# Expert stage of a graph and feed-forward kernel: first weights copied to fixed places, and a ring of four output buffers

## The chip, the cores and the metric

The kernel runs on one core of a Trainium2 chip. The metric is the device time of one execution in microseconds (us). The kernel before takes 2433.99 us, the median of three runs (2428.54 to 2436.15).

The engines are named as the profile names them: PE is TensorE's matmul and PEld its weight load, DVE is VectorE, ACT is ScalarE, POOL is GpSimd, SP is the engine that issues most DMAs. A name with a q behind it (SPq, POOLq) is the instruction queue of that engine.

## The reference

Two parts run one after the other on 3125 nodes with 256 features each.

```
x = x + gnn(layernorm(x))            # 4 layers of a relational graph network, 100000 edges
x = x + ffn(layernorm(x))            # a mixture of 8 experts, 2 for each node

def ffn(x):                          # E = 8 experts, D = 256, H = 512
    xn = layernorm(x) * gamma + beta
    top_vals, top_idx = top_k(xn @ Wr + br, 2)
    w = softmax(top_vals)
    for e in range(E):
        h   = gelu(xn @ W1[e] + b1[e])          # 256 -> 512
        y_e = h @ W2[e] + b2[e]                 # 512 -> 256
        y  += y_e * (w of expert e, 0 where the node did not choose it)
```

Only the second part, and in it only the experts and what follows them, is touched here.

## The kernel before, in words

The graph layers and the routing fill the first 2140 us. The router gives every chosen pair of node and expert a row in a table XG in device memory, sorted by expert; an expert's rows are padded up to a multiple of 128. A row holds the node's normalized features as a high and a low float16 half and, behind them, the number of the row of the output table YG to which its result goes. Padding rows hold number 0, and row 0 of YG is read by nobody; node n owns rows 1 + 2n and 2 + 2n.

The expert stage works on NB = 56 blocks of 128 rows. Each block has one expert, known only on the chip, so its weights are addressed through a register (`bass.ds(at, ...)`). Both weight tables lie in SBUF for all 8 experts, 2048 float16 columns each: W1HL and W2HL. For a block b the engines do this:

- SP loads the 128 rows of XG into XB (4 buffers, L1224). It waits until the block four before has been transposed and until its output row numbers have been copied.
- PE `turn(b)` transposes the four 128x128 pieces (L2104); ACT `turned(b)` takes them to SBUF (L1361).
- PE `up(b)` (L2115) makes 24 matmuls of 128x128 with weights from W1HL. Here the weights are the stationary operand, and its address is dynamic.
- ACT applies Gelu in four pieces (L1375) and makes the high half of the result (L1381). DVE makes the low half (L2080, semaphore `hl`).
- PE `down(b)` (L2130) makes 12 matmuls with 256 columns. Stationary is the hidden value, at a fixed address; W2HL is the moving operand, at a dynamic address.
- DVE `down_evac(b)` (L2067) scales, adds b2 and writes YB, which has 2 buffers.
- POOL (L1424) writes YB to the rows of YG by an indirect DMA, whose row numbers DVE has copied into IDX (L2078, 4 columns).

The order on each engine is written out by hand. PE does turn(b+1), up(b), down(b-2). ACT does turned(b+1), Gelu(b), high half(b). DVE does the row numbers of b, the low half of b, the evacuation of b-2. POOL issues the write of b when `ybv` says that the evacuation is done and, from the second on, when the write of b-1 has landed (`yb0` or `yb1`). DVE takes the row numbers of b only when the write of b-4 has landed, and evacuates b-2 only when b-4 has.

When all writes have landed, SP reads YG back, 25 tiles of 125 nodes (L1229, two DMAs each), DVE adds the two weighted results of each node to X (L1563, L1566), and ACT's queue stores the tile. DVE waits for the loads in groups of tiles: 0 and 1, then four at a time from 2 to 21, then 22 to 24.

The program holds a second kernel for other graphs (the Dense classes and functions). It isn't executed with this input.

Of the kernel before, what the change touches and what calls it, by code (L numbers as in the profile page):

```python
# [7 lines left out]
F32 = mybir.dt.float32  # L8
# [652 lines left out]
class Memory:  # L661


    def __init__(self, nc, ctx, c):
# [3 lines left out]
        def dram(name, shape, dt):  # L668
            return nc.dram_tensor(f"n_{name}", shape, dt).ap()
# [448 lines left out]
def sync_program(e, a, c, m, s):  # L1118
# [271 lines left out]
def gpsimd_program(e, a, c, m, s):  # L1390
# [66 lines left out]
def vector_program(e, done, a, c, m, s):  # L1457
# [257 lines left out]
def tensor_program(e, a, c, m, s):  # L1715
# [12 lines left out]
    for what, l, i in c.order:  # L1728
# [53 lines left out]
        elif what == "rd":  # L1782
# [233 lines left out]

def blocks_vector(e, q, c, m, s):

    bq, bt, ti = m.bc[0:TN], m.bt, m.ti

# [38 lines left out]
    def expert(b, w):  # L2059
        return e.snap(regs[w][b // GB % 2][b % GB], min_val=0, max_val=(E8 - 1) * (1, 256)[w])  # L2060

    def down_evac(b):
        e.wait_ge(s["dn"], b + 1)
        e.wait_ge(s["b2"], 16) if b == 0 else None
        if b >= 2:
            e.wait_ge(s[f"yb{b % 2}"], 16 * (b // 2))
        e.scalar_tensor_tensor(m.YB[:, b % 2, :], m.bank(3 + b % 3, 0, D), m.FSC[:, 1, bass.ds(expert(b, 0), 1)],  # L2067
                               m.B2F[:, bass.ds(expert(b, 1), D)], ALU.mult, ALU.add).then_inc(s["ybv"], 1)

    for b in range(NB + 2):  # L2070
        if b < NB:
            if b % GB == 0:
                for w in range(2):
                    e.reg_load(regs[w][b // GB % 2], ti[0:1, (2, 4)[w], b:b + GB])
            e.wait_ge(s[f"xb{b % 4}"], 16 * (b // 4 + 1))
            if b >= 4:
                e.wait_ge(s[f"yb{b % 2}"], 16 * ((b - 4) // 2 + 1))
            e.tensor_copy(m.IDX[:, b % 4:b % 4 + 1], m.XB[:, b % 4, 2 * D:RW].bitcast(I32)).then_inc(s["idx"], 1)  # L2078
            e.wait_ge(s["hh"], b + 1)
            e.scalar_tensor_tensor(m.HHL[:, b % 3, 1, :], m.H[:, b % 2, :], m.fsc[:, bass.ds(expert(b, 0) + 24, 1)],  # L2080
                                   m.HHL[:, b % 3, 0, :], ALU.mult, ALU.subtract).then_inc(s["hl"], 1)
        if b >= 2:
            down_evac(b - 2)


def experts(e, c, m, s, n_whl):
    e.wait_ge(s["posd"], c.routes)
# [7 lines left out]
    def expert(b):  # L2095
        return e.snap(regs[b // GB % 2][b % GB], min_val=0, max_val=(E8 - 1) * 2048)
# [10 lines left out]
    def up(b):  # L2107
        e.wait_ge(s["xbt"], b + 1)
        if b >= 3:
            e.wait_ge(s["gl"], b - 2)  # L2110
        at = expert(b)
        for k4 in range(4):
            for k in range(2):
                for w, x in ((0, 0), (0, 1), (1, 0)):
                    ins = e.matmul(m.bank(b % 3, 128 * k4, 128),  # L2115
                                   m.W1HL[:, bass.ds(at + (1024 * k + 512 * w + 128 * k4), 128)],
                                   m.XBT[:, b % 2, 128 * (2 * x + k):128 * (2 * x + k) + 128],
                                   start=(k == 0 and w + x == 0), stop=(k == 1 and w == 1))
        ins.then_inc(s["up"], 1)
# [196 lines left out]
class DenseMemory:  # L2316


    def __init__(self, nc, ctx, c):
# [169 lines left out]
def dense_sync(e, a, c, m, s):  # L2489
# [104 lines left out]
def dense_scalar(e, a, c, m, s):  # L2594
# [317 lines left out]
def dense_vector(e, a, c, m, s):  # L2912
# [122 lines left out]
def dense_tensor(e, a, c, m, s):  # L3035
# [207 lines left out]
```

## Time and profile before

| what | us |
|---|---|
| median of the runs shown | 2433.99 |
| span of the profiled execution, first to last instruction | 2411.0 |
| PE busy | 2037.9 (85%) |
| DVE busy | 1593.9 (66%) |
| ACT busy | 800.7 (33%) |
| POOL busy | 1363.9 (57%) |
| mean granted TensorE clock | 0.940 of full speed |
| first and last start of L2115, the up matmuls | 2146.7 and 2351.2 |
| first and last start of L1424, the output writes | 2162.1 and 2370.7 |
| first start of L1229, the reading back | 2373.9 |

The profile states no time of its own for the profiled execution other than the span. The runs shown are 23 us longer than the span: that is what lies before the first and behind the last instruction, and the change doesn't touch it.

A busy share is an average over the whole kernel, and this change touches the last 265 us. So the views that matter are the timeline, the chain of waits and the busy times of that stretch. Each waiting instruction is put down to the one that ended last before it; where an engine is never put down as waiting, its own pace is the limit.

### The profile page before, as it was taken

How to read it: one execution, taken by the hardware profiler on the slowest of the kernel's cores; microseconds unless marked ns; L12 is line 12 of the kernel's file. 1: busy time of each engine (PE TensorE's matmuls, PEld its weight loads, DVE VectorE, ACT ScalarE, POOL GpSimd, SP SyncE). 2: the span in 40 equal slices, each digit the busy share in tenths (PEclk: the TensorE clock that was granted, in tenths of full speed). 3: DMA queues.
4: the chain of work that ended last, by engine and by line, in shares of the span. 5: the costliest groups of instructions: out<-in, count | busy, mean ns of one | idle time of the engine just before them, and what ended most of it. 6: DMA issues, size and time to landing. Idle time of an engine off the chain costs nothing. (4 is left out here: it accounts for less than half of the span.)

```text
span 2411.0 us, 48597 instructions
## 1 busy us (share of the span) xinstructions
PE 2037.9 (85%) x16548; PEld 1310.3 (54%) x16548; DVE 1593.9 (66%) x5383; ACT 800.7 (33%) x1632; POOL 1363.9 (57%) x1344
## 2 busy tenths in 40 slices
PE   0576998999988989889999999889999998559990
PEld 0334655665555556556655565554665655348780
DVE  5986877877866567676646776763677777543334
ACT  1665656665541111111111221210122112137770
POOL 2034554646450777777467777764777777722230
PEclk9988999999999999999999999999999998669995
DMA  5599554535553787776579777756776564332225
GB/s 154 156 276 296 149 147 127 163 118 186 148 153 88 257 235 257 238 222 209 179 244 270 243 255 236 249 175 216 260 239 207 184 205 118 98 99 72 70 73 174
DMA packets 215194, 448.63 MB, mean 186 GB/s; under 512 B 42478, under 2 KB 138722, under 8 KB 213287
## 3 DMA queue, kind: packets, MB, share of 16 engines
q1 hardware_dynamic: 136023, 261.82, 35.1%
q0 software_dynamic: 67168, 172.52, 23.7%
q10 hardware_dynamic: 11760, 11.08, 1.7%
q8 instruction: 147, 2.41, 0.4%
q14 instruction: 96, 0.79, 0.1%
HBM read 344.26 MB, written 100.70 MB: 185 GB/s over the span
## 5 line engine op out<-in xcount | busy, mean ns | idle before, releaser
L1402 POOL DMA_INDIRECT n_BIG<-n_xd,n_SIDX x1200 | 1226.5, 1022 | 768.6 <-PE n_PS L1891 307.7
L1870 PE MATMUL n_PS<-n_BIG 125*128 125x500 f16 x4400 | 1059.8, 377 | 14.7 <-DVE n_BIG L1536 12.3
L1870 PEld LDWEIGHTS n_PS<-n_BIG 125*128 125x128 f16 x4400 | 392.6, 98 | 361.4 <-issue 15.4
L1891 PE MATMUL n_PS<-n_OW,n_BIG 128*128 128x116 f16 (+24 forms) x4800 | 352.7, 207 | 112.6 <-DMA n_BIG<-n_xd,n_SIDX 110.8
L1891 PEld LDWEIGHTS n_PS<-n_OW,n_BIG 128*128 128x128 f16 x4800 | 290.2, 99 | 278.7 <-DMA n_BIG<-n_xd,n_SIDX 147.4
L1911 PE MATMUL n_PS<-n_BIG,n_tabs 128*128 128x256 f16 x2400 | 295.8, 283 | 0.0
L1582 DVE TENSOR_TENSOR n_ST<-n_PS,n_INVB 128x500 f32<-128x500 f32 x200 | 200.3, 1043 | 125.1 <-issue 65.3
L1911 PEld LDWEIGHTS n_PS<-n_BIG,n_tabs 128*128 128x128 f16 x2400 | 244.7, 102 | 36.9
L1491 DVE TENSOR_SCALAR n_OW<-n_io,n_tabs 128x116 f16<-128x116 f16 (+24 forms) x1200 | 213.1, 270 | 57.6 <-PE n_PS L1891 57.4
L1608 DVE SCALAR_TENSOR_TENSOR n_U<-n_PS,n_cw,n_BI 125x256 f32<-125x256 f32 x100 | 48.1, 481 | 256.5 <-PE n_PS L1911 256.0
L1304 ACT ACTIVATE n_U<-n_U 125x256 f32<-125x256 f32 x100 | 41.4, 414 | 517.5 <-DVE n_U L1618 487.2
L1293 ACT ACTIVATE n_tabs<-n_ST 128x1000 f16<-128x1000 f32 x100 | 103.7, 1037 | 325.5 <-DVE n_ST L1582 295.4
L1277 ACT ACTIVATE n_BIG<-n_PS 128x500 f16<-128x500 f32 x275 | 150.5, 577 | 136.1 <-PE n_PS L1841 135.4
L1841 PE MATMUL n_PS<-n_BIG,n_tabs 128*128 128x400 bf16 (+4 forms) x576 | 134.8, 338 | 28.2 <-DVE n_tabs L1483 10.9
L1424 POOL DMA_INDIRECT n_yg<-n_BIG,n_IDX x56 | 59.9, 1069 | 172.8 <-DMA n_yg<-n_BIG,n_IDX 146.8
L1478 DVE TENSOR_SCALAR n_BIG<-n_io,n_tabs 128x400 bf16<-128x400 f16 (+4 forms) x576 | 147.9, 309 | 8.1 <-PE n_PS L1841 8.1
L1504 DVE TENSOR_TENSOR n_tabs<-n_ST,n_tabs 128x1000 f16<-128x1000 f32 x100 | 119.7, 1197 | 30.5 <-ACT n_tabs L1293 30.4
L2115 PE MATMUL n_PS<-n_BIG 128*128 128x128 f16 x1344 | 114.7, 226 | 0.3
L1284 ACT ACTIVATE n_XT<-n_PS 128x500 f16<-128x500 f16 x100 | 58.5, 586 | 155.3 <-PE n_PS L1753 155.2
L1258 ACT ACTIVATE n_tabs<-n_io,n_tabs 128x125 bf16<-128x125 f16 x288 | 91.2, 390 | 44.6 <-PE n_PS L1841 44.3
L2115 PEld LDWEIGHTS n_PS<-n_BIG 128*128 x1344 | 92.5, 99 | 18.4 <-issue 2.2
L1375 ACT ACTIVATE n_BIG<-n_PS,n_B1T,n_FSC 128x128 f32<-128x128 f32 x224 | 84.4, 457 | 43.7 <-PE n_PS L2115 41.2
(275 smaller groups left out, 2219.4 us busy)
## 6 DMA issues: line engine op xcount, KB each, us to landing
n_BIG<-n_a SPq DMA_DIRECT2D x160, 625.0 KB, 5.5
n_a<-n_BIG SPq DMA_DIRECT2D x11, 3125.0 KB, 12.2
n_xg<-n_tabs SPq DMA_DIRECT2D x53, 481.9 KB, 10.1
n_INVB<-n_ind SPq DMA_DIRECT2D x100, 250.0 KB
n_BIG<-n_xd,n_SIDX POOLq DMA_INDIRECT x1200
n_BIG<-in_L_ffn_W_dram SPq DMA_DIRECT2D x32, 512.0 KB, 4.7
n_xd<-n_BIG SPq DMA_DIRECT2D x75, 112.0 KB
n_whl<-n_BIG SPq DMA_DIRECT2D x16, 512.0 KB
```

Source lines behind the costliest of these rows:

```text
L1277: e.activation(rows[:, :, 20 * g:20 * g + 20], m.bank(4 + c.unit_of["block", i], 0, W).rearrange("p (q k) -> p k q", k=T), ACT.Copy).then_ ...
L1293: e.activation(m.SH[i % 2 if l else 0][:, 0, :, :, 0:TN], m.ST, ACT.Copy).then_inc(s["shi"], 1)
L1402: e.indirect_dma_start(m.GR[:, g % GS, :], None, m.XD[l % 2][:, :], bass.IndirectOffsetOnAxis(ap=m.SIDX[:, i:i + 1], axis=0)).then_inc(s[f ...
L1478: e.tensor_scalar(m.OC[i % S][:, at], m.io[:, at], m.VS[:, i:i + 1], None, ALU.is_equal).then_inc(s["oc"], 1)
L1491: e.tensor_scalar(c.window(m, w)[0], m.io[:, 0:c.width[w]], m.SCOL[:, w:w + 1], None, ALU.is_equal).then_inc(s["win_made"], 1)
L1504: e.tensor_tensor(lo, m.ST, hi, ALU.subtract).then_inc(s["slo"], 1)
L1582: ins = e.tensor_tensor(m.ST[:, h], m.bank(2 * p + h, 0, W).rearrange("p (n r) -> p r n", r=R), m.INVB[:, k, :].rearrange("p (n r) -> p r ...
L1841: e.matmul(m.bank(4 + c.unit_of["block", g])[:, at], m.OS[b % 3][:, i % 4, :], m.OC[i % S][:, at], start=(j == 0), stop=(j + 1 == c.groups ...
L1870: ins = e.matmul(m.bank(2 * p + h, 0, W), m.xps[l % 2][0:TN, part, D * k + 128 * h:D * k + 128 * h + 128], m.RA[0:TN, c.slot_of(n), W * (k ...
L1891: ins = e.matmul(m.bank(2 * p + h, at, c.width[q]), m.GR[:, g % GS, D * part + 128 * h:D * part + 128 * h + 128], ow, start=False, stop=Fa ...
L1911: ins = e.matmul(out, sums[:, x, h, r, :], m.WH[:, l % 2, w, h, r, :], start=False, stop=(x == 1 and h == 1 and r == R - 1))
L2115: ins = e.matmul(m.bank(b % 3, 128 * k4, 128), m.W1HL[:, bass.ds(at + (1024 * k + 512 * w + 128 * k4), 128)], m.XBT[:, b % 2, 128 * (2 * x ...
```

## The change

It has four parts, all in the expert stage and in what follows.

1. A ring W1R of W1S = 4 places with fixed addresses, in SBUF that the graph layers have left. DVE copies the 2048 columns of a block's first weights from W1HL to place b % 4 (`w1_copy`), three blocks before the loop and in it, and then at the start of iteration b for block b+2. PE's `up(b)` waits for the copy (`w1_put`) and reads the ring. The copy waits until the up matmuls of the place's last user are done.
2. YB has YS = 4 buffers, in other memory, with four semaphores. POOL no longer waits for the write of b-1; DVE evacuates block b when the write of b-4 has landed. The row numbers still wait for the write of b-4.
3. YG has 4 spare rows ahead of the nodes' rows. A padding row's number becomes b % 4 (a maximum with b % 4), by one instruction in place of the copy.
4. The groups of tiles that DVE waits for at the end begin at tiles 0, 3, 8, 13 and 19: five groups, where it had seven.

```diff
+LOADED = (3, 8, 13, 19)
+YS = 4
+W1S = 4
...
+        self.W1R = BIG[:, 0:2048 * W1S].rearrange("p (b h) -> p b h", b=W1S)
...
-        self.YB = xpf[:, 5120:5632].rearrange("p (b d) -> p b d", b=2)
+        self.YB = raf[:, 4096:4096 + YS * D].rearrange("p (b d) -> p b d", b=YS)
...
 for b in range(NB):                                   # POOL
     e.wait_ge(s["ybv"], b + 1)
-    if b:
-        e.wait_ge(s[f"yb{(b - 1) % 2}"], 16 * ((b - 1) // 2 + 1))
     e.indirect_dma_start(m.YG[:, :], bass.IndirectOffsetOnAxis(ap=m.IDX[:, b % 4:b % 4 + 1], axis=0),
-                         m.YB[:, b % 2, :], None).then_inc(s[f"yb{b % 2}"], 16)
+                         m.YB[:, b % YS, :], None).then_inc(s[f"yb{b % YS}"], 16)
...
+    def w1_copy(b):                                   # DVE
+        if b % GB == 0:
+            e.reg_load(wide[b // GB % 2], ti[0:1, 1, b:b + GB])
+        if b >= W1S:
+            e.wait_ge(s["up"], b - W1S + 1)
+        at = e.snap(wide[b // GB % 2][b % GB], min_val=0, max_val=(E8 - 1) * 2048)
+        e.tensor_copy(m.W1R[:, b % W1S, :], m.W1HL[:, bass.ds(at, 2048)]).then_inc(s["w1_put"], 1)
+
+    if ring:
+        e.wait_ge(s["whl"], 16 * 12)
+        for b in range(W1S - 2):
+            w1_copy(b)
     for b in range(NB + 2):
         if b < NB:
+            if ring and b + W1S - 2 < NB:
+                w1_copy(b + W1S - 2)
...
             if b >= 4:
-                e.wait_ge(s[f"yb{b % 2}"], 16 * ((b - 4) // 2 + 1))
-            e.tensor_copy(m.IDX[:, b % 4:b % 4 + 1], m.XB[:, b % 4, 2 * D:RW].bitcast(I32)).then_inc(s["idx"], 1)
+                e.wait_ge(s[f"yb{b % ys}"], 16 * ((b - 4) // ys + 1))
+            rows_of = m.XB[:, b % 4, 2 * D:RW].bitcast(I32)
+            if ring:
+                e.tensor_scalar(m.IDX[:, b % 4:b % 4 + 1], rows_of, float(b % YS), None, ALU.max).then_inc(s["idx"], 1)
...
-        at = expert(b)                                # PE, up(b)
+        if ring:
+            e.wait_ge(s["w1_put"], b + 1)
...
+                    col = 1024 * k + 512 * w + 128 * k4
                     ins = e.matmul(m.bank(b % 3, 128 * k4, 128),
-                                   m.W1HL[:, bass.ds(at + (1024 * k + 512 * w + 128 * k4), 128)],
+                                   m.W1R[:, b % W1S, col:col + 128] if ring else m.W1HL[:, bass.ds(at + col, 128)],
```

On PE, the rows of one block from its transposes to its second matmuls. L2096 works out the block's register, ISA are register instructions, BIG holds the weights and PS is PSUM. Before:

```order
L2104 MATMUL n_PS<-n_idh,n_tabs 128x128 x3
L2096 ISA [waits gl,xbt]
L2115 MATMUL n_PS<-n_BIG 128x128 x2
L2115 ISA
L2115 MATMUL n_PS<-n_BIG 128x128
L2115 ISA
L2115 MATMUL n_PS<-n_BIG 128x128 x2
```

The pattern goes on until 24 matmuls are through. Now:

```order
L2132 MATMUL n_PS<-n_idh,n_tabs 128x128 x3
L2147 MATMUL n_PS<-n_BIG 128x128 [waits w1_put,gl,xbt]
L2147 MATMUL n_PS<-n_BIG 128x128 x23
L2124 ISA [waits hl]
L2162 MATMUL n_PS<-n_BIG 128x256
L2162 ISA
```

The 15 register instructions between the up matmuls are gone, and the one ahead of them; those of the down matmuls stay. A wait on `w1_put` has come in.

On DVE, one iteration of the loop, from the row numbers to the next row numbers. Before:

```order
L2078 COPY n_IDX<-n_tabs 128x1 [waits yb1,xb1]
L2060 ISA [waits hh]
L2080 SCALAR_TENSOR_TENSOR n_BIG<-n_BIG,n_fi 128x512
L2060 ISA [waits yb1,dn]
L2067 REGISTER_ALU
L2067 SCALAR_TENSOR_TENSOR n_BIG<-n_PS,n_FSC,n_BIG 128x256
L2078 COPY n_IDX<-n_tabs 128x1 [waits yb0,xb2]
```

Now:

```order
L2104 TENSOR_SCALAR n_IDX<-n_tabs 128x1 [waits yb1,xb1]
L2068 ISA [waits hh]
L2108 SCALAR_TENSOR_TENSOR n_BIG<-n_BIG,n_fi 128x512
L2068 ISA [waits dn]
L2075 REGISTER_ALU
L2075 SCALAR_TENSOR_TENSOR n_BIG<-n_PS,n_FSC,n_BIG 128x256
L2082 TENSOR_LOAD n_BIG
L2085 ISA [waits up]
L2086 COPY n_BIG<-n_BIG 128x2048
L2104 TENSOR_SCALAR n_IDX<-n_tabs 128x1 [waits yb2,xb2]
```

Between the evacuation and the next row numbers stands the copy of 128x2048, with the load of four block offsets (L2082) once in four blocks. In the first blocks the evacuation waits for no write.

## Rows read from the trace of the kernel before

**Rows 1.** Busy time by stretch: us, then PE, PEld, DVE, ACT, POOL, clock, DMA share, GB/s

```profile
2155.30:2349.40 194.10, 191.56 (x2119) 157.44 (x2118) 67.64 (x156) 144.79 (x322) 53.67 (x51) 1.00 0.23 71
```

**Rows 2.** Waits from 2155.3 to 2349.4: engine, line, releaser, us in total, times, longest

```profile
POOL n_yg L1424 <- DMA n_yg<-n_BIG,n_IDX: 130.7, 49, 4.4
...
PE n_PS L2104 <- DMA n_tabs<-n_xg: 0.6, 1, 0.6
```

**Rows 3.** DMA issues from 2155.3 to 2349.4: count, median us to landing

```profile
n_yg<-n_BIG,n_IDX POOLq DMA_INDIRECT x51, 2.7
```

**Rows 4.** Timeline, 2298 to 2310: start, us, engine, line, operation

```profile
2299.14 1.76 PEld L2115 LDWEIGHTS n_PS<-n_BIG 128*128 x24
...
2301.06 1.22 PEld L2130 LDWEIGHTS n_PS<-n_BIG 128*128 128x128 f16 x12
...
2304.66 1.50 PE L2130 MATMUL n_PS<-n_BIG 128*128 x12
...
2306.22 1.91 PE L2115 MATMUL n_PS<-n_BIG 128*128 128x128 f16 x24
```

**Rows 5.** Timeline, 2154.5 to 2162.2, the third and fourth block

```profile
2155.33 1.51 ACT L1375 ACTIVATE n_BIG<-n_PS,n_B1T,n_FSC 128x128 f32<-128x128 f32 x4 [1.64 <-PE n_PS L2115]
2155.38 2.12 PE L2115 MATMUL n_PS<-n_BIG 128*128 128x128 f16 x24
2156.98 0.72 ACT L1381 ACTIVATE n_BIG<-n_BIG,n_fi 128x512 f16<-128x512 f32 x1
...
2157.87 0.75 DVE L2080 SCALAR_TENSOR_TENSOR n_BIG<-n_BIG,n_fi 128x512 f16<-128x512 f32 x1 [3.69 <-ACT n_BIG L1381]
...
2158.81 1.16 PEld L2115 LDWEIGHTS n_PS<-n_BIG 128*128 x20
```

**Rows 6.** DVE's groups by shape, whole kernel: busy us, mean ns | idle before

```profile
L1478 DVE TENSOR_SCALAR n_BIG<-n_io,n_tabs 128x500 bf16<-128x500 f16 x186 | 64.6, 351 | 8.1 <-PE n_PS L1841 8.1
...
L1478 DVE TENSOR_SCALAR n_BIG<-n_io,n_tabs 128x100 bf16<-128x100 f16 x83 | 20.1, 249 | 0.0
...
L1519 DVE SCALAR_TENSOR_TENSOR n_BIG<-n_BIG,n_wb 128x2048 f16<-128x2048 f32 x4 | 9.4, 2350 | 4.4 <-ACT n_BIG L1298 4.4
...
L2078 DVE COPY n_IDX<-n_tabs 128x1 int32<-128x1 int32 x56 | 8.6, 154 | 116.8 <-DMA n_yg<-n_BIG,n_IDX 113.2 <-DMA n_tabs<-n_xg 3.6
```

**Rows 7.** Line 1491, whole kernel: count: ns min/median/max, first and last start

```profile
L1491 DVE TENSOR_SCALAR n_OW<-n_io,n_tabs x1200: 210/244/691, 120.5 to 2090.6; 128x104 f16<-128x104 f16 x13, 128x124 f16<-128x124 f16 x11, 128x92 f16<-128x92 f16 x9, 128x120 f16<-128x120 f16 x9
```

**Rows 8.** Line 1402, whole kernel, the same columns

```profile
L1402 POOL DMA_INDIRECT n_BIG<-n_xd,n_SIDX x1200: 940/946/3237, 113.8 to 2104.2; - x172
```

**Rows 9.** Timeline, 2348.9 to 2352, the last block's up matmuls

```profile
2349.45 2.01 PE L2115 MATMUL n_PS<-n_BIG 128*128 128x128 f16 x24
```

**Rows 10.** Timeline, 2350 to 2411, from the last Gelu to the last tile

```profile
2351.63 1.51 ACT L1375 ACTIVATE n_BIG<-n_PS,n_B1T,n_FSC 128x128 f32<-128x128 f32 x4 [0.97 <-PE n_PS L2115]
...
2356.02 0.75 DVE L2080 SCALAR_TENSOR_TENSOR n_BIG<-n_BIG,n_fi 128x512 f16<-128x512 f32 x1
...
2356.93 1.74 PE L2130 MATMUL n_PS<-n_BIG 128*128 x12 [2.35 <-DVE n_BIG L2080]
...
2373.88 21.83 SPq L1229 DMA_DIRECT2D n_BIG<-n_yg  x50
...
2394.74 0.48 DVE L1563 SCALAR_TENSOR_TENSOR n_X<-n_BIG,n_INVA,n_X 125x256 f32<-125x256 f32 x1 [0.57 <-DMA n_BIG<-n_yg]
...
2398.95 0.48 DVE L1563 SCALAR_TENSOR_TENSOR n_X<-n_BIG,n_INVA,n_X 125x256 f32<-125x256 f32 x1 [0.46 <-DMA n_BIG<-n_yg]
...
2404.97 0.48 DVE L1566 SCALAR_TENSOR_TENSOR n_X<-n_BIG,n_INVA,n_X 125x256 f32<-125x256 f32 x1
```

**Rows 11.** Chain of waits, 2344 to 2411: start, us, what

```profile
2355.82 0.71 issue
2356.52 4.99 DMA n_yg<-n_BIG,n_IDX
...
2370.69 3.12 DMA n_yg<-n_BIG,n_IDX
```

More of the change, by code:

```diff
@@ L59 @@
 xo0 xo1 x1 xn xh_hi xh_lo xh_iota xh rxt xnt lg sm2 rexp sel rpos posd pos_made
-cnt_mm bi_made ti_made b2 xbt_mm xbt up gl hh hl dn ybv idx y_last out""".split()
+cnt_mm bi_made ti_made b2 w1_put xbt_mm xbt up gl hh hl dn ybv idx y_last out""".split()
 NEARS += [f"slot{i}" for i in range(6)] + [f"row{i}" for i in range(GS)] + [f"scat{i}" for i in range(XHS)]
-NEARS += [f"xb{i}" for i in range(4)] + [f"yb{i}" for i in range(2)] + [f"g{i}" for i in range((T + 1) // 4 + 1)]
+NEARS += [f"xb{i}" for i in range(4)] + [f"yb{i}" for i in range(YS)] + [f"g{i}" for i in range(len(LOADED) + 1)]
 DENSES = """padded edges x_in consts pool_const ev r0 gathered gp_tr vs b1 b1_tr ln hi0 xp oc os slot_free evac
@@ L677, in __init__ @@
         self.MW = dram("mw", (L, 128), F32)
-        self.YG = dram("yg", (1 + 2 * N, D), F32)
+        self.YG = dram("yg", (YS + 2 * N, D), F32)
+        self.y_rows = self.YG[YS:, :]
         self.AD = dram("a", (c.TD, 128, T * W), F16)
@@ L891, in prep_gpsimd @@
     k.did(e.memset(m.onef[:, :], 1.0))
-    k.did(e.iota(m.rows[:, :], [[1, 2]], base=1, channel_multiplier=2))
+    k.did(e.iota(m.rows[:, :], [[1, 2]], base=YS, channel_multiplier=2))
     k.did(e.memset(m.mh[:, :], -0.5))
@@ L1224, in sync_program, with wait_outputs_ready, load_group @@
         e.dma_start(m.XB[:, b % 4, :], m.XG[bass.ds(row, 128), :]).then_inc(s[f"xb{b % 4}"], 16)
-    wait_outputs_ready(e, s)
+    wait_outputs_ready(e, s, YS)
     for t in range(T):
         for p, n in ROWS:
-            e.dma_start(m.two(t)[p:n].rearrange("p j d -> p (j d)"), gathered(m, t)[p:n]).then_inc(s[f"g{(t + 2) // 4}"], 16)
+            e.dma_start(m.two(t)[p:n].rearrange("p j d -> p (j d)"), gathered(m, t)[p:n]).then_inc(s[f"g{load_group(t)}"], 16)
     e.wait_ge(s["out"], 32 * T)
-def wait_outputs_ready(e, s):
+def wait_outputs_ready(e, s, ys):
     e.wait_ge(s["dn"], NB)
-    for i in range(2):
-        e.wait_ge(s[f"yb{i}"], 16 * (NB // 2))
+    for i in range(ys):
+        e.wait_ge(s[f"yb{i}"], 16 * (NB // ys))
+def load_group(t):
+    return sum(1 for first in LOADED if t >= first)
 def gathered(m, t):
-    return m.YG[1:1 + 2 * N, :].rearrange("(n j) d -> n (j d)", j=2)[TN * t:TN * t + TN]
+    return m.y_rows.rearrange("(n j) d -> n (j d)", j=2)[TN * t:TN * t + TN]
 def scalar_program(e, a, c, m, s):
@@ L1557, in vector_program @@
             places(e, q, m, s, i)
-    blocks_vector(e, q, c, m, s)
+    blocks_vector(e, q, c, m, s, True)
     for t in range(T):
-        e.wait_ge(s[f"g{(t + 2) // 4}"], 32 * sum(1 for i in range(T) if (i + 2) // 4 == (t + 2) // 4))
+        e.wait_ge(s[f"g{load_group(t)}"], 32 * sum(1 for i in range(T) if load_group(i) == load_group(t)))
         both, n = m.two(t), c.place[L - 1, t] - (L - 1) * T
@@ L1792, in tensor_program @@
             ins.then_inc(s["rpos"], 1)
-    experts(e, c, m, s, 12)
+    experts(e, c, m, s, 12, True)
 def unit_free(e, c, s, name):
@@ L2014, in route_vector, with blocks_vector @@
         q.did(e.tensor_tensor(m.PW[0:TN, t, 1:2], m.sm[0:TN, 3:4], m.PW[0:TN, t, 0:1], ALU.mult))
-def blocks_vector(e, q, c, m, s):
-    bq, bt, ti = m.bc[0:TN], m.bt, m.ti
+def blocks_vector(e, q, c, m, s, ring):
+    bq, bt, ti, ys = m.bc[0:TN], m.bt, m.ti, YS if ring else 2
     def rows(k):
@@ L2064, in down_evac @@
         e.wait_ge(s["b2"], 16) if b == 0 else None
-        if b >= 2:
-            e.wait_ge(s[f"yb{b % 2}"], 16 * (b // 2))
-        e.scalar_tensor_tensor(m.YB[:, b % 2, :], m.bank(3 + b % 3, 0, D), m.FSC[:, 1, bass.ds(expert(b, 0), 1)],
+        if b >= ys:
+            e.wait_ge(s[f"yb{b % ys}"], 16 * (b // ys))
+        e.scalar_tensor_tensor(m.YB[:, b % ys, :], m.bank(3 + b % 3, 0, D), m.FSC[:, 1, bass.ds(expert(b, 0), 1)],
                                m.B2F[:, bass.ds(expert(b, 1), D)], ALU.mult, ALU.add).then_inc(s["ybv"], 1)
+    wide = [[e.alloc_register(f"bw{c.TD}_{g}_{i}") for i in range(GB)] for g in range(2)] if ring else []
+    def w1_copy(b):
[9 more added lines that the diff above has]
+            w1_copy(b)
     for b in range(NB + 2):
         if b < NB:
+            if ring and b + W1S - 2 < NB:
+                w1_copy(b + W1S - 2)
             if b % GB == 0:
@@ L2083, in blocks_vector, with experts @@
             down_evac(b - 2)
-def experts(e, c, m, s, n_whl):
+def experts(e, c, m, s, n_whl, ring):
     e.wait_ge(s["posd"], c.routes)
@@ L2110, in up @@
             e.wait_ge(s["gl"], b - 2)
-        at = expert(b)
+        if ring:
+            e.wait_ge(s["w1_put"], b + 1)
+        else:
+            at = expert(b)
         for k4 in range(4):
@@ L2335, in __init__ @@
         self.YG = dram("yg", (1 + 2 * N, D), F32)
+        self.y_rows = self.YG[1:, :]
         self.AD = dram("a", (TD, 128, T * W), F16)
@@ L2718, in dense_scalar @@
                      scale=m.fsc[:, bass.ds(expert(b, 0) + 24, 1)]).then_inc(s["hh"], 1)
-    wait_outputs_ready(e, s)
+    wait_outputs_ready(e, s, 2)
     for t in range(0, T, 2):
@@ L3022, in dense_vector @@
             route_vector(e, q, c, m, s, what, i)
-    blocks_vector(e, q, c, m, s)
+    blocks_vector(e, q, c, m, s, False)
     for t in range(T):
@@ L3120, in dense_tensor @@
                      ).then_inc(s["rpos"], 1)
-    experts(e, c, m, s, 13)
+    experts(e, c, m, s, 13, False)
 def dense_tile_step(e, c, m, s, l, j, dense_free):
```

4 lines of the change are left out of this document (3 added, 1 removed).

## The prediction

> **What bounds the kernel now.** I began with the busy times by stretch, then the waits of the same stretch, then single blocks in the timeline, and last the chain of waits.
>
> From the third block's up matmuls at 2155.38 [rows 5] to the last block's at 2349.45 [rows 9] there are 53 blocks in 194.07 us, 3.66 us a block. In that stretch PE is busy 191.6 of 194.1 us, at the full clock [rows 1], and waits for data 0.6 us in all, once [rows 2]. So PE's own pace sets these blocks. The chain of waits names the output writes instead, and POOL does wait 130.7 us for them [rows 2]. Both are true. The writes go one at a time and fall behind PE in the course of the stretch, since a landing can take 4.99 us where 2.7 is the median [rows 3, 11]. PE doesn't feel it, because the hidden values that it needs are due two blocks later. The debt is paid behind the last block: from its up matmuls (2349.45) to the start of the reading back (2373.88) it takes 24.43 us [rows 9, 10].
>
> So there are two limits, with one part of the change for each, and a third place, the end.
>
> **The fixed weights (PE).** Down and transposes take 1.56 us (2304.66 to 2306.22) [rows 4], so the up matmuls take 3.66 - 1.56 = 2.10 us on average. They are 24 pairs of weight load and matmul, with 16 register instructions of PE's queue among them. Where the queue has run ahead, the old kernel shows what a pair costs without these: 20 loads in 1.16 us, the last of them 0.10 long, is 1.06 / 19 = 0.056 us each [rows 5]. Fixed addresses should give this for all: 24 x 0.056 = 1.34 us. There is also the gap ahead of the down matmuls. The last up load starts at 2299.14 + 1.76 - 0.10 = 2300.80, the first down load at 2301.06 [rows 4], 0.26 us later, which is 0.20 more than one pair. This is the queue working out the next register when it is not ahead of the array. With no register instruction in 24 pairs it will be ahead, so I take 0 of it, and keep 0.20 as the other end. For the load of block offsets once in four blocks, which no row isolates, I add 0.03 a block. The new block is 1.56 + 1.34 + 0.03 = 2.93 us, between 2.90 and 3.13. The gain is 53 x (3.66 - 2.93) = 38.7 us, between 28 and 40.
>
> Is another engine late next? ACT is busy 144.8 / 53 = 2.73 us a block [rows 1]. That is just below 2.93, and the floor if PE did better: 49 us gained at most. For DVE see below. POOL needs 53.7 / 51, 1.05 us a write [rows 1, 3].
>
> **The copies (DVE).** DVE is busy 67.6 / 53 = 1.28 us a block [rows 1] and gets 56 copies of 2048 float16 columns. No row has this copy. The nearest is the float16 comparison of L1478: 351 ns at 500 columns, 249 at 100, so 0.255 ns a column [rows 6]. By it the copy takes 249 + 1948 x 0.255 = 746 ns. The other end is L1519, with as many columns but float32 input, 2350 ns [rows 6]. I take 0.75, since type and single tensor input agree. DVE then needs 2.03 us a block, hidden under PE's 2.93. If the copy took 2.35, DVE would need 3.63 and the whole PE gain would be gone (a rival below). The three copies ahead of the loop, 2.2 us, fit into the 3.6 us in which DVE's first row numbers wait for the rows of XG [rows 6].
>
> The new wait on `w1_put` has the up and down matmuls queued behind it. A copy starts about when the low half and the evacuation of the iteration before are over. Counted from the end of up(b-1): Gelu and high half 2.5 us, low half and evacuation 1.2, copy 0.75, so 4.5. PE wants it at up(b+2), 3 x 2.93 - 1.34 = 7.4 us after the same point. 2.9 us to spare, cost nothing; without that cover it would be added once, not for each block.
>
> **The writes in flight (POOL, DVE).** POOL's wait for the last write goes. DVE's wait for the write of b-4 ahead of the row numbers stays. From there it is 0.15 us (numbers), then low half and evacuation 1.2, at most 0.7 until POOL starts [rows 11], landing 2.7: 4.8 us for two blocks, 2.4 for one, below 2.93. A landing of 5 us adds 2.3 to that, which reaches PE only if it is two blocks late. That SP's loads of XG hang on the row numbers costs nothing either: PE waited 0.6 us for them while the numbers were delayed by the writes; now they come sooner. The maximum in place of the copy of row numbers is one small DVE instruction for another, 0.15 us [rows 6]. Spare rows: 0, bounded by the 2.3 us between a long and a median landing, for the last write alone.
>
> Within the stretch this part gains nothing by itself, but it has to be there: with single writes (2.7 us, and 0.71 until the next starts [rows 3, 11]) POOL couldn't go below 3.4 us a block.
>
> Behind the last block it gains directly. Of the 24.43 us there remain: up matmuls to the end of the last one 24 x 0.056 + 0.17 = 1.51; Gelu starts 0.17 later (2349.45 + 2.01 to 2351.63) [rows 9, 10]; Gelu to high half 1.65 (2155.33 to 2156.98); high to low half 0.89 [rows 5]; low half to down matmuls 0.91 (2356.02 to 2356.93); down 1.74; evacuation 0.6, since an operation of its kind and width takes 0.48 [rows 10]; write 3.12 [rows 11]; 0.07 to the reading back. Sum 10.6 us, gain 13.8, between 11 (a landing of 5 us and one more us of queueing) and 14.
>
> **The groups at the end.** DVE takes a group of tiles when its last tile is in. The tiles up to 17 are in at 2394.74 and those up to 21 at 2398.95 [rows 10], 1.05 us a tile, so tile 24 is in at 2402.1. Now the last group has 6 tiles instead of 3. A tile costs (2404.97 + 0.48 - 2398.95) / 7 = 0.93 us [rows 10], so DVE ends at 2402.1 + 5.6 = 2407.7, not at 2405.45: 2.2 us lost. Fewer stores have gone out by then, which leaves the loads a little faster. I take 2.0, between 0 and 3.
>
> **Sum.** -38.7 - 13.8 + 2.0 = -50.5 us. The span of 2411.0 becomes 2360.5; with the 23 us around it that is 2383.5, and I forecast 2384.
>
> **The rivals.**
>
> *PE keeps its gap* (0.20 a block), or the pair stays at 0.063: 3.13 us a block, 2434 - 28.1 - 13.8 + 2 = 2394. For it: the register instruction ahead of the down matmuls is still there. Against: 20 loads in a row keep 0.056 us in rows 5, so the queue can be that far ahead.
>
> *DVE and POOL exclude each other.* Every copy starts as the evacuation ends, which is when POOL issues the write. Float16 comparisons of DVE (L1491) ran while POOL issued its gathers: 244 ns median but 691 at most [rows 7], and POOL's gathers 946 median but 3237 at most [rows 8]. So they do disturb each other, mostly by little. If each copy waited for a whole issue, DVE would need 2.03 + 1.1 = 3.13 us a block, and its loads of offsets come on top, about 3.2: 2434 - 24 - 13.8 + 2 = 2398. The Trainium skill says just this (SBUF — State Buffer, SBUF: two separate sides): VectorE in a two-port mode and GpSimd hold a port pair exclusively for the whole instruction. The median of L1491 speaks against "the whole", its maximum for a part.
>
> *The copy is slow* (2.35 us): DVE sets 3.63 a block, the stretch gains 2 us, the end about 12, in all 2434 - 2 - 12 + 2 = 2422.
>
> *Slower than before:* the slow copy, held up by each issue of POOL as well. DVE then needs 1.28 + 2.35 + 1.1 = 4.73 us a block, 53 x 1.07 = 57 us more, less the end's 12: 2481. The kernel gets slower from the point where 53 x (block - 3.66) exceeds the 11.8 us of the end, a block of 3.88 or a copy of 2.6 us with its waits. Against it: two unfavourable ends at once.
>
> *The writes still go one at a time*, since one queue carries them. Then POOL's 3.4 us a block bind: 2434 - 14 - 6 + 2 = 2416. Against it: the gathers of L1402, which POOL issues in the same way, start 1.66 us apart on average (1200 between 113.8 and 2104.2 [rows 8]), with POOL's other work among them; that is less than one landing.
>
> **How the numbers follow.** Forecast 0.60, PE's gap 0.16, mutual exclusion 0.09, single writes 0.04, slow copy 0.05, slower 0.03, no change 0.03. A measurement of this kernel tells a change from none at about 0.3%, 7 us. All but the last two are faster by more: 0.94 faster, 0.03 the same, 0.03 slower. The range goes from 2375 (tail at its best, PE halfway to ACT's floor) to 2402, past the gap and the exclusion.
>
> **What would show it.** In the profile after: 24 up weight loads in about 1.4 us, up-to-up distance of 2.9 us, PE still without waits and at the full clock; copies of 128x2048 at about 0.75 us; ACT nearly without idle time; from the last up matmuls to the reading back 10.6 us instead of 24.4; DVE's last pair of operations 5 to 6 us behind its last wait. The forecast is wrong if PE waits on `w1_put` or `hl`, if the copies take over 1.6 us, if up loads stay above 0.07 us apart, or if POOL's write still starts after the landing of the one before.

## The result, and the profile after

The changed kernel takes 2374.07 us, the median of four runs (2371.73 to 2378.72), against 2431.26 of the kernel before (2427.49 to 2436.15). The ratio is 0.9763 with a 95% interval of 0.9742 to 0.9783, so the change gains 57 us where 50.5 were forecast, and the time lies 1 us below the range. The forecast of 2384 was counted from 2433.99, the median of three runs of the kernel before; the median of four is 2.7 us lower. In later rounds the ratio was 0.9749 (0.9714 to 0.9784).

The busy times of the changed kernel, from the third block's up matmuls to the last block's (us, then PE, PEld, DVE, ACT, POOL, clock, DMA share, GB/s), answer to [rows 1]:

```profile
2169.70:2322.00 152.30, 152.30 (x2120) 144.69 (x2118) 96.72 (x212) 143.37 (x321) 59.97 (x51) 1.00 0.30 91
```

The same 53 blocks take 152.3 us instead of 194.1, 2.87 us a block, and PE is busy all the time. ACT is busy 143.4 us, 94% of it. The waits of the same stretch answer to [rows 2]:

```profile
POOL n_yg L1432 <- DVE n_BIG L2075: 106.1, 51, 22.0
DVE n_BIG L2108 <- ACT n_BIG L1391: 57.7, 49, 8.5
DVE n_IDX L2104 <- DMA n_yg<-n_BIG,n_IDX: 6.1, 5, 2.3
ACT n_BIG L1385 <- PE n_PS L2147: 0.6, 1, 0.6
```

POOL now waits for evacuations and no longer for landings. PE's matmuls don't appear. The timeline of one block (start, us, engine, line) answers to [rows 4, 5]:

```profile
2221.33 0.68 DVE L2086 COPY n_BIG<-n_BIG 128x2048 f16 x1
...
2221.70 1.16 POOL L1432 DMA_INDIRECT n_yg<-n_BIG,n_IDX  x1 [1.71 <-DVE n_BIG L2075]
2221.76 1.38 PEld L2147 LDWEIGHTS n_PS<-n_BIG 128*128 128x128 f16 x24
...
2223.10 1.25 PEld L2162 LDWEIGHTS n_PS<-n_BIG 128*128 128x128 f16 x12
2223.15 1.47 PE L2162 MATMUL n_PS<-n_BIG 128*128 x12
...
2224.63 1.38 PEld L2147 LDWEIGHTS n_PS<-n_BIG 128*128 128x128 f16 x24
```

The 24 up loads are (1.38 - 0.10) / 23 = 0.056 us apart, and from one block's up loads to the next block's it is 2.87 us. The first down load comes 0.06 us after the last up load (2221.76 + 1.38 - 0.10 = 2223.04): the gap of [rows 4] is gone. The copy takes 0.68 us, and POOL's issue begins in the middle of it.

That the register instructions held up the loads can be read from the two kernels. These are the instructions of the up matmuls in one block (count, ns min/median/max, first and last start), before and then after; PEldq is the queue of the weight loads, and after it has no such row:

```profile
L2115 PEld LDWEIGHTS n_PS<-n_BIG x24: 95/96/99, 2302.6 to 2304.4; 128*128 x24
L2115 PEldq FUSED_REGOPS  x15: 46/46/46, 2302.5 to 2304.3; - x15
```

```profile
L2147 PEld LDWEIGHTS n_PS<-n_BIG x24: 97/98/98, 2221.8 to 2223.0; 128*128 128x128 f16 x24
```

Before, 15 register instructions start over 1.8 us, some 0.13 us apart, and the loads among them take as long. The 24 pairs by themselves need 24 x 0.056 = 1.34 us.

The last blocks in the timeline answer to [rows 9 to 11]:

```profile
2322.05 1.44 PEld L2147 LDWEIGHTS n_PS<-n_BIG 128*128 128x128 f16 x24
...
2329.05 0.97 POOL L1432 DMA_INDIRECT n_yg<-n_BIG,n_IDX  x1 [0.30 <-issue]
2330.33 0.97 POOL L1432 DMA_INDIRECT n_yg<-n_BIG,n_IDX  x1 [0.30 <-issue]
2333.55 22.55 SPq L1234 DMA_DIRECT2D n_BIG<-n_yg  x50
...
2366.21 0.48 DVE L1574 SCALAR_TENSOR_TENSOR n_X<-n_BIG,n_INVA,n_X 125x256 f32<-125x256 f32 x1
```

From the last up loads to the reading back it is 11.5 us, not 24.5. Two writes stand one behind the other with 1.28 us between their starts.

### The profile page after: what moved, and what is told of

It reads as the page before. It is cut to its first block and busy times, and to the rows that moved or that the text cites. A ratio compares the mean times of both kernels' runs of the same rounds, so it can differ in the third digit from the quotient of the medians.

```text
span 2372.3 us, 47774 instructions
## 1 busy us (share of the span) xinstructions
PE 1997.1 (84%) x16548; PEld 1298.6 (55%) x16548; DVE 1622.5 (68%) x5439; ACT 799.1 (34%) x1632; POOL 1365.3 (58%) x1344
## 5 line engine op out<-in xcount | busy, mean ns | idle before, releaser
L1432 POOL DMA_INDIRECT n_yg<-n_BIG,n_IDX x56 | 64.8, 1158 | 111.8 <-DVE n_BIG L2075 111.2
L1915 PE MATMUL n_PS<-n_RL,n_XT 128*128 128x256 f16 x600 | 92.6, 296 | 8.1 <-DVE n_tabs L1512 7.6
L1849 PEld LDWEIGHTS n_PS<-n_BIG,n_tabs 128*128 128x128 bf16 x576 | 55.3, 102 | 73.0 <-DVE n_BIG L1486 22.2
L2147 PE MATMUL n_PS<-n_BIG 128*128 128x128 f16 x1344 | 86.5, 222 | 0.0
```

Source lines behind the costliest of these rows:

```text
L1849: e.matmul(m.bank(4 + c.unit_of["block", g])[:, at], m.OS[b % 3][:, i % 4, :], m.OC[i % S][:, at], start=(j == 0), stop=(j + 1 == c.groups ...
L2147: ins = e.matmul(m.bank(b % 3, 128 * k4, 128), m.W1R[:, b % W1S, col:col + 128] if ring else m.W1HL[:, bass.ds(at + col, 128)], m.XBT[:, b ...
```

## The experiments

Stage times, read from the traces, tell these kernels apart better than totals. The kernel before ran between 2413.6 and 2441.8 us over all its runs. In its three profiles the expert stage starts at 2146.6, 2167.9 and 2150.4 us; in the two of the changed kernel at 2162.2 and 2155.1. The columns: the first two blocks, the 53 blocks from the third to the last (and us a block), from the last up loads to the reading back, and from there to the start of DVE's last operation.

| kernel | first two | 53 blocks | end | reading back |
|---|---|---|---|---|
| before, first profile | 8.6 | 194.1 (3.66) | 24.5 | 31.1 |
| before, second | 7.2 | 198.7 (3.75) | 24.8 | 30.6 |
| before, third | 7.2 | 199.0 (3.75) | 24.1 | 30.6 |
| after, first | 7.5 | 152.3 (2.87) | 11.5 | 32.7 |
| after, second | 8.9 | 152.7 (2.88) | 11.5 | 32.0 |
| weights only | 7.1 | 205.6 (3.88) | 26.2 | 30.7 |
| writes only | 7.2 | 191.7 (3.62) | 12.0 | 32.6 |
| slow copy | 7.1 | 179.6 (3.39) | 11.7 | 32.9 |
| two products | 6.9 | 146.3 (2.76) | 12.0 | 32.3 |
| both weights fixed | 8.5 | 153.3 (2.89) | 12.0 | 34.1 |
| groups at 8, 14, 19, 23 | 9.3 | 152.8 (2.88) | 11.5 | 32.8 |
| groups at 5, 11, 17, 22 | 7.1 | 152.0 (2.87) | 11.5 | 32.3 |
| before with the new groups | 8.5 | 202.4 (3.82) | 24.3 | 32.3 |

**The kernel before, twice more.** No edit.

> The kernel before, unchanged, a second profile of it. Theory 1 (the earlier stages vary from one execution to the next): the time is that of the kernel before within 0.2%, the span lies 2 us below the time of its own execution, and the expert stage starts up to 16 us later than in the first profile (2146.7 us), near 2162 as in the changed kernel. Theory 2 (the change made the graph layers slower or faster too): the expert stage starts at 2147 us within 3 us again. In both, the 53 blocks from the third to the last take 194 us and the end behind them 24 us.

Measured: 0.9993 (0.9971 to 1.0015), profiled at 2437.47 us with a span of 2435.4. Theory 1 holds: the stages ahead vary by 20 us from one execution to the next, and not with the change. It didn't foresee that the 53 blocks take 4.6 us more.

> A third profile of the kernel before. The expert stage starts anywhere between 2146 and 2170 us. Theory 1 (in this kernel PE is ahead of the writes by a little only): the 53 blocks take 194 to 199 us and the difference from 194 is what PE waits for rows of XG. Theory 2 (PE's own pace varies): the time differs without waits of PE.

Measured: 2419.94 us, one run. The stretch in this third profile, and PE's wait in it:

```profile
2157.60:2356.50 198.90, 194.28 (x2118) 157.68 (x2116) 67.71 (x158) 144.73 (x321) 53.72 (x50) 0.99 0.22 69
```

```profile
PEld n_PS L2104 <- DMA n_tabs<-n_xg: 4.7, 8, 1.3
```

PE is idle 4.6 us here, where it was 2.5 us in [rows 1]. The weight loads wait 4.7 us for rows of XG. These are the same waits in the first profile, in the second, and in the kernel before with the new groups of tiles (below), which has the same blocks and takes 202.4 us for them:

```profile
PEld n_PS L2104 <- DMA n_tabs<-n_xg: 1.3, 3, 0.9
PEld n_PS L2104 <- DMA n_tabs<-n_xg: 5.1, 7, 1.0
PEld n_PS L2109 <- DMA n_tabs<-n_xg: 8.0, 13, 1.3
```

The longer the stretch, the longer they wait, and in the kernel with the writes alone, below, they don't wait for these rows at all. XG's rows wait for the row numbers, and these wait for the writes. So the single writes reach PE a little in every execution, and by 3 to 7 us more in three of the four. The clock adds little: it is at the lower level in the first 2.4 us of the stretch here and in the first 1.3 us in the first profile, which is half a us of PE's time.

```profile
2157.60:2160.00 2.40, 2.40 (x26) 2.40 (x24) 0.34 (x2) 2.25 (x6) 0.00 (x0) 0.50 0.12 22
2155.30:2156.60 1.30, 1.30 (x15) 1.30 (x14) 0.00 (x0) 1.27 (x4) 0.00 (x0) 0.50 0.46 103
```

About 1 us of the difference isn't settled.

**Each half alone.** The weights only: as changed, but two output buffers and spare rows, seven groups, and this:

```diff
-YS = 4
+YS = 2
...
         e.wait_ge(s["ybv"], b + 1)
+        if b:
+            e.wait_ge(s[f"yb{(b - 1) % YS}"], 16 * ((b - 1) // YS + 1))
```

> The fixed weights alone: copies by VectorE, but two output buffers (two spare rows), each write waiting for the one before, and the seven groups of tiles. Theory 1 (two limits, one behind the other): the writes now bind. Their chain ran 208.6 us for 55 writes in the first profile, 3.79 us each, and stays so; PE waits for the low halves or VectorE for writes, the block distance is 3.5 to 3.8 us, and the end is later by what PE is ahead: 0 to 4 us faster than before. Theory 2 (PE's pace is the only limit, the chain of waits names a bystander): 53 x 0.79 = 42 us faster, the block distance 2.87 us.

Measured: 1.0024 (1.0005 to 1.0044), a little slower than before. The waits of the 53 blocks:

```profile
POOL n_yg L1434 <- DMA n_yg<-n_BIG,n_IDX: 127.1, 48, 4.2
DVE n_IDX L2106 <- DMA n_yg<-n_BIG,n_IDX: 100.5, 48, 3.7
...
PE n_PS L2134 <- DMA n_tabs<-n_xg: 22.3, 42, 1.7
...
PE n_PS L2164 <- DVE n_BIG L2110: 13.7, 11, 1.6
```

The writes now bind, as theory 1 had it: PE waits 36 us, for XG's rows and for low halves, both of which hang on landings. That it is slower than before was not expected. DVE's copies lengthen POOL's issue, and with single writes each issue stands in the chain. Here is the group of the writes with copies and single writes, and behind it the one of the kernel before, with single writes and no copies, and the one of the kernel with the writes alone, with neither (busy us, mean ns | idle):

```profile
L1434 POOL DMA_INDIRECT n_yg<-n_BIG,n_IDX x50 | 68.9, 1378 | 151.1 <-DMA n_yg<-n_BIG,n_IDX 127.1 <-DVE n_BIG L2077 21.3 <-issue 2.7
```

```profile
L1424 POOL DMA_INDIRECT n_yg<-n_BIG,n_IDX x51 | 54.8, 1074 | 156.8 <-DMA n_yg<-n_BIG,n_IDX 130.7 <-DVE n_BIG L2067 23.1 <-issue 2.9
```

```profile
L1432 POOL DMA_INDIRECT n_yg<-n_BIG,n_IDX x52 | 50.5, 970 | 156.3 <-DVE n_BIG L2075 156.3
```

So the copies cost an issue 0.30 us here (1378 against 1074 ns). The median from issue to landing goes from 2.7 [rows 3] to 3.0 us, and from the first write to the last it takes 222 us (2182.8 to 2404.9), where the three profiles of the kernel before have 209 to 214.

The writes only: `experts(..., False)` on PE, and without the copies on DVE.

```diff
-    if ring:
-        e.wait_ge(s["whl"], 16 * 12)
-        for b in range(W1S - 2):
-            w1_copy(b)
...
-            if ring and b + W1S - 2 < NB:
-                w1_copy(b + W1S - 2)
```

> The writes alone: four output buffers, four spare rows, no wait of the write for the one before, and the five groups of tiles; the first weights are read at addresses from a register as before, and no copies are made. Theory 1: the block distance stays 3.66 us, since PE's register instructions set it; the end behind the last up matmuls shrinks from 24.4 to about 12 us, and the groups cost 1.6: 10 to 12 us faster. Theory 2 (the writes are the limit, as the chain of waits says): 40 us or more faster with block distances below 3 us.

Measured: 0.9929 (0.9904 to 0.9954), 16 us faster by the medians. The end shrinks to 12.0 us and the blocks keep 3.62 us. PE's matmuls wait 0.2 us for data in the stretch: this is the pace of its own queue with register instructions, 0.05 to 0.14 us below the three profiles of the kernel before. That is what the expectation missed. Theory 2 falls.

**The whole again, in the same rounds.**

> The changed kernel, unchanged, in the same rounds as its two halves. 55 to 58 us faster than before. Theory 1: the block distance is 2.87 us, that is 24 x 0.056 + 4 x 0.056 + 12 x 0.109, nothing but the matmuls' own time; the gain is more than the sum of the two halves (12 to 16 us) by 40 us. Theory 2: the halves add up.

Measured: 2368.20 us, 0.9749 (0.9714 to 0.9784), 59 us faster than before. By the medians the halves give +7 and -16 us; the sum of -9 leaves 50 us that only both together bring. One part moves the limit to the place that the other one clears.

**A slow copy.** The same result by an operation that reads the weights twice.

```diff
-        e.tensor_copy(m.W1R[:, b % W1S, :], m.W1HL[:, bass.ds(at, 2048)]).then_inc(s["w1_put"], 1)
+        e.scalar_tensor_tensor(m.W1R[:, b % W1S, :], m.W1HL[:, bass.ds(at, 2048)], 1.0, m.W1HL[:, bass.ds(at, 2048)],
+                               ALU.mult, ALU.max).then_inc(s["w1_put"], 1)
```

> The changed kernel with each copy made by a scalar_tensor_tensor that reads the weights twice (max of 1 x w and w), at one element a cycle: 2048 columns, about 2.2 us instead of 0.68. The result is the same. Theory 1 (a copy is free until VectorE is full): VectorE then needs 1.28 + 2.2 and its waits, 3.5 to 3.6 us a block against PE's 2.87, so the block distance becomes 3.5 to 3.6 and PE waits for w1_put or the low half; the end behind the last block stays near 11.5 us. In all 20 to 25 us faster than the kernel before. Theory 2 (VectorE and the issuing GpSimd exclude each other for a whole instruction): 4.6 us a block or more, and slower than before by 30 us or more.

Measured: 0.9862 (0.9839 to 0.9886), 32 us faster than before by the medians, where 20 to 25 were expected. The groups of the stretch:

```profile
L1432 POOL DMA_INDIRECT n_yg<-n_BIG,n_IDX x51 | 141.2, 2769 | 53.7 <-DVE n_BIG L2075 53.7
L2086 DVE SCALAR_TENSOR_TENSOR n_BIG<-n_BIG 128x2048 f16 x53 | 120.9, 2281 | 0.1
```

DVE sets the pace at 3.39 us, 0.1 to 0.2 less than expected, because one operation starts some 0.08 us before the one ahead of it ends. The interesting row is POOL's: an issue takes 2.77 us instead of 0.97. The timeline shows what it waits for. First one block of this kernel, then one of the kernel with the weights alone:

```profile
2285.32 2.28 DVE L2086 SCALAR_TENSOR_TENSOR n_BIG<-n_BIG 128x2048 f16 x1
2285.68 2.77 POOL L1432 DMA_INDIRECT n_yg<-n_BIG,n_IDX  x1 [0.55 <-DVE n_BIG L2075]
```

```profile
2290.36 1.37 POOL L1434 DMA_INDIRECT n_yg<-n_BIG,n_IDX  x1 [2.28 <-DMA n_yg<-n_BIG,n_IDX]
2290.53 0.48 DVE L2077 SCALAR_TENSOR_TENSOR n_BIG<-n_PS,n_FSC,n_BIG 128x256 f32<-128x256 f32 x1
...
2290.92 0.68 DVE L2088 COPY n_BIG<-n_BIG 128x2048 f16 x1
```

With the slow copy the issue ends 0.85 us behind DVE's operation (2288.45 and 2287.60), and in the changed kernel too (2222.86 and 2222.01, from the timeline above), though one operation is three times as long as the other. So the issue stands still until DVE's operation is over. The exclusion is real, but it is POOL that pays, and POOL has slack as long as several writes are in flight. The Trainium skill (SBUF — State Buffer, SBUF: two separate sides) lets whichever starts first hold the port pair while the other blocks. The timeline agrees where DVE is first, in these two kernels. It doesn't agree where POOL is first: with the weights alone the copy starts 0.56 us behind the issue, at the end of the evacuation as it always does, takes its 0.68 us, and the issue ends 0.13 us behind it. No run here shows DVE blocked for a whole issue; in the changed kernel the copy has a mean of 683 ns, below the 746 of the estimate.

**Two products of three** in the up matmuls. This leaves out the product of the high weights with the low features.

```diff
-                for w, x in ((0, 0), (0, 1), (1, 0)):
+                for w, x in ((0, 0), (1, 0)) if ring else ((0, 0), (0, 1), (1, 0)):
```

> The changed kernel without the product of the high weights with the low features: the up matmuls are 16 instead of 24. This leaves out part of the computation. Theory 1: PE's array then needs 16 x 0.056 + 4 x 0.056 + 12 x 0.109 = 2.43 us a block, but ScalarE's own sum of one block without waits is 2.75 us, so the distance is 2.75 to 2.80, and 4 to 6 us are gained on the changed kernel. Theory 2 (ScalarE has slack that its busy time hides): 2.43 us a block, 23 us gained on the changed kernel.

Measured: 2.76 us a block, with ACT's own 2.75 expected. In the 146.3 us ACT waits for PE 0.8 us, once, while PE's weight loads now wait 4.9 us for ACT and 11.5 for rows of XG. So ACT is the next limit, 0.11 us below PE, and the rows of XG are not far behind it. The total, 0.9733 (0.9706 to 0.9760) against before, can't show the 6 us.

**Both weights at fixed places.**

```diff
+        self.W2R = BIG[:, 10240:10240 + 4096].rearrange("p (b h) -> p b h", b=2)
...
+        if ring and b < NB:
...
+            e.tensor_copy(m.W2R[:, b % 2, :], m.W2HL[:, bass.ds(at, 2048)]).then_inc(s["h2"], 1)
...
-                               m.W2HL[:, bass.ds(at + (512 * k4 + 256 * w), D)],
+                               m.W2R[:, b % 2, c2:c2 + D] if ring else m.W2HL[:, bass.ds(at + c2, D)],
```

> The changed kernel with the second weights too at fixed places (a ring of 2, one more copy of 2048 columns on VectorE a block), so that no register instruction is left on PE in the loop; four groups of tiles at the end, from 0, 5, 12 and 20, since semaphores are short. Theory 1 (PE is bound by the array, 24 x 0.056 + 4 x 0.056 + 12 x 0.109 = 2.87 us): the block distance stays 2.87 us, or rises slightly where VectorE, now at 2.6 us a block, is late; total within 0.3% of the changed kernel. Theory 2 (the remaining register instructions of the down matmuls still cost): below 2.80 us a block, 4 us or more gained on the changed kernel.

Measured: 2.89 us a block, 0.9769 (0.9744 to 0.9793) against before. Nothing is gained. The 12 down matmuls take (1.47 - 0.27) / 11 = 0.109 us each (0.27 us is the length of a single one), 1.31 us in all, and there are 7 register instructions among them (392 in 56 blocks of the changed kernel); at the 0.13 us read above these are an estimated 0.9 us, and hidden already. PE is bound by the array.

**Other groups at the end.** The edit is LOADED alone.

> The changed kernel with the five groups of tiles beginning at 0, 8, 14, 19 and 23 instead of 0, 3, 8, 13 and 19, so that the last group has 2 tiles instead of 6. Theory 1 (the end is the last load's landing plus the last group's work at 0.93 us a tile): from the start of the reading back to VectorE's last operation 30 to 31 us instead of 32.1 to 32.7, 1.5 to 2.5 us gained. Theory 2 (VectorE's 25 tiles bind, since the first group starts later): 23.3 us after the first group's landing at 8 tiles, 36 us, and 3 us or more lost.

> The changed kernel with the groups of tiles beginning at 0, 5, 11, 17 and 22. Theory (two bounds: the first group's landing plus 25 tiles of 0.91 us, and the last tile's landing, some 28 us after the start, plus the last group): about 7.7 + 22.8 = 30.5 by the first, 28 + 2.7 = 30.7 by the second, so 30.7 to 31.5 us from the start of the reading back to VectorE's last operation, against 32.0 to 32.7 in the changed kernel. A gain of about 1 us, too little to be seen in the total. Rival (it is the amount of stores in flight that delays the last loads): 32 us again.

Measured: 32.8 and 32.3 us for the reading back, 0.9761 (0.9740 to 0.9782) and 0.9755 (0.9725 to 0.9785). Both expectations of a gain are wrong, and so are the 36 us of the first one's theory 2, though its mechanism is right: with 8 tiles in the first group DVE waits once, and then its 25 tiles bind:

```profile
DVE n_X L1571 <- DMA n_BIG<-n_yg: 14.3, 1, 14.3
```

DVE starts 10.3 us after the first load's issue, not 12.7 as that theory had it, and its last operation starts 22.5 us after that. With 5 tiles first it starts at 7.4 us, and waits 1.59 and 0.65 us more.

> The kernel before with nothing but the five groups of tiles from 0, 3, 8, 13 and 19. From the start of the reading back to VectorE's last operation 32.0 to 32.7 us as in the changed kernel, against 30.6 to 31.1 with seven groups, so the groups alone account for the 1.5 us; the rival is that the new place of YG's rows (4 spare rows, so another offset) costs them: then 31 us.

Measured: 32.3 us in one run, so the 1.6 us are the groups' and not those of YG's new rows. DVE's waits in this kernel (start, us, engine, line, and in brackets the idle time before):

```profile
2394.70 0.48 DVE L1568 SCALAR_TENSOR_TENSOR n_X<-n_BIG,n_INVA,n_X 125x256 f32<-125x256 f32 x1 [12.09 <-DMA n_BIG<-n_yg]
2399.56 0.48 DVE L1568 SCALAR_TENSOR_TENSOR n_X<-n_BIG,n_INVA,n_X 125x256 f32<-125x256 f32 x1 [2.02 <-DMA n_BIG<-n_yg]
2404.76 0.48 DVE L1568 SCALAR_TENSOR_TENSOR n_X<-n_BIG,n_INVA,n_X 125x256 f32<-125x256 f32 x1 [0.53 <-DMA n_BIG<-n_yg]
2411.34 0.48 DVE L1568 SCALAR_TENSOR_TENSOR n_X<-n_BIG,n_INVA,n_X 125x256 f32<-125x256 f32 x1 [1.90 <-DMA n_BIG<-n_yg]
```

There are four waits for five groups. DVE doesn't wait for the last one, which begins at tile 19: it is in by the time that DVE gets to it. The first three of the kernel before (the others are in [rows 10]):

```profile
2378.22 0.48 DVE L1563 SCALAR_TENSOR_TENSOR n_X<-n_BIG,n_INVA,n_X 125x256 f32<-125x256 f32 x1 [11.35 <-DMA n_BIG<-n_yg]
2382.30 0.48 DVE L1563 SCALAR_TENSOR_TENSOR n_X<-n_BIG,n_INVA,n_X 125x256 f32<-125x256 f32 x1 [2.16 <-DMA n_BIG<-n_yg]
2386.58 0.48 DVE L1563 SCALAR_TENSOR_TENSOR n_X<-n_BIG,n_INVA,n_X 125x256 f32<-125x256 f32 x1 [0.53 <-DMA n_BIG<-n_yg]
```

From the first load DVE starts after 4.3 us there and waits 3.7 us later on; with the five groups it starts after 5.1 us and waits 4.5.

That padding rows all go to one row with several writes in flight was not tried, since two writes would then be under way to the same row with no order between them.

No version beat the changed kernel by what can be measured.

## Why the prediction was right in its mechanism and wrong in its size

By the profiles' means (three of before, two of after) the stage changes by 152.5 - 197.2 = -44.7 us in the 53 blocks, 11.5 - 24.5 = -13.0 at the end, 32.4 - 30.8 = +1.6 in the reading back and 8.2 - 7.7 = +0.5 in the first two blocks. The sum is -55.6 us, a ratio of 0.977, inside both intervals. What is beyond it (57 and 59 us) is within what the stages ahead vary. With the 202.4 us of the kernel with the new groups as a fourth value of the blocks before, it would be -57 us.

- **The block, a term of the sum: wrong in size, -38.7 forecast and -44.7 measured.** This is the step that failed: the term was sized wrong on both of its sides. "The new block is 1.56 + 1.34 + 0.03 = 2.93 us, between 2.90 and 3.13": it is 2.87, below the lower bound. The 1.34 was exact. The 1.56 for down and transposes is 1.53 now (2223.10 to 2224.63), which is 12 x 0.109 + 4 x 0.056: the 12 down matmuls take 1.47 us where [rows 4] have 1.50. Why they ran slower before isn't shown. The 0.03 for the block offsets doesn't exist: the distance is 2.87 us in blocks with the load of offsets and without. That is 0.06 us a block, 3 us. The other 3 us are in the block before: 3.66 us came from one execution, two more show 3.75 and a fourth 3.82; the mean of the first three is 3.72.
- **"PE waits for data 0.6 us in all" and therefore sets the pace alone:** right for that execution, too strong for the kernel. In three others the weight loads wait 5 to 8 us for XG's rows, behind the writes. The cover between PE and the writes was a thin one, and one profile can't show how thin.
- **The gap ahead of the down matmuls** was taken at nothing, and is gone. The rival that kept it falls.
- **The copies:** 746 ns estimated, 683 measured, hidden as forecast. The slow copy set the pace through DVE, as its rival had it, at 3.39 instead of 3.63 us.
- **The exclusion of DVE and POOL:** the rival had the payer wrong. POOL's issue grows, DVE's copies don't, and the block stays at PE's.
- **"This part gains nothing by itself, but it has to be there":** right. The weights alone come out at 1.0024. The writes alone also gained a little, 0.05 to 0.14 us a block. The "3.4 us a block" for single writes was too low: in the first profile already, 55 writes take 208.6 us, 3.79 each (first and last start of L1424), and with the weights alone it is 4.04.
- **The end:** 13.0 instead of 13.8 us. The forecast left out that the last two writes are issued one behind the other, 1.28 us apart: the last evacuation ends at 2329.52 and its write is issued at 2330.33.
- **The groups:** +1.6 against +2.0, near for a wrong reason. DVE's loss lies in the earlier waits (0.7 us) and in the later start (0.8 us), not in the last group of six. The sign "DVE's last pair of operations 5 to 6 us behind its last wait" didn't come: in the changed kernel its last wait ends at 2355.61 and the last operation starts at 2366.21.
- **"The 23 us around" the span:** wrong. The second profile has a span of 2435.4 and a time of 2437.47, so 2 us lie around it. So the first profile was of an execution some 20 us quicker than the runs shown; its expert stage starts 21 us earlier than in the second profile. The 23 us themselves moved no term, but they hid how much executions differ.
- **The range:** its low end of 2375 is explained as "tail at its best, PE halfway to ACT's floor". That is a block of 2.83 us, and 2434 - 44 - 14 + 2 = 2378, or 2376 with the groups at nothing; so the low end already allowed a new block faster than the one that came. What carried the time past it lies in the kernel before: its mean block of 3.72 instead of 3.66 us (3 us), and its median of 2431.26 instead of 2433.99 (2.7 us). The time is 0.9 us outside, less than either. Which side of the edge it fell on is chance; that the gain was put 6 us too low isn't.

## What to carry to other kernels

Where an engine is busy all the time and the chain of waits names another, ask how far apart the two paces are: here 3.62 us a block for PE and 3.8 to 3.9 us for the writes, which may fall behind for a while, so that either part alone moved the time by less than 1% and both together by 2.4%. Matmuls at computed addresses pay for their register instructions only where these take longer than the array: 15 of them among 24 matmuls of 128 columns did, 7 among 12 of 256 columns did not. Take the floor of an engine from its own instructions, not from a difference of measured averages: from the rows of the kernel before it would have been 24 x 0.056 + 4 x 0.056 + 12 x 0.112 = 2.91 us. With the 0.109 that a down matmul takes in the changed kernel the sum is the measured 2.87; as this 0.109 was read afterwards, it says what binds PE now and forecasts nothing.

## What was not expected of the hardware

- POOL's issue of an indirect write takes 0.97 us alone, 1.18 us beside DVE copies of 0.68 us, and 2.77 us beside DVE operations of 2.28 us that read two tensors in SBUF. With single writes it takes 1.07 us without copies and 1.38 with them. DVE's operations start and end as without POOL, also when the issue began first; one copy of 771 ns among 56, in the kernel with the weights alone, is the only exception.
- A float16 copy of 2048 columns takes 683 ns, with a source address from a register, less than the 746 that were worked out from a float16 comparison.
- The time of one and the same program varies by 28 us over 2430. Between its quickest and its slowest profile there are 24 us, and 21 of them lie ahead of the expert stage.
